# Moving the low part of a late expert weight on VectorE, in a fused graph layer and mixture of experts

## The reference, cut to what matters

```
deg = max((adj != 0).sum(-1), 1);  dinv = rsqrt(deg)
x = x + relu(((dinv * (adj + I) * dinv) @ ln(x) + ln(x)) @ Wg + bg)    # 4096 nodes, 256 features
xf = ln(x)
w, idx = top_k(softmax(xf @ Wr + br), 2);  w = w / w.sum()             # 16 experts
for e in range(16):
    h = gelu(xf @ W1[e] + b1[e])            # 256 -> 512
    y += combine[:, e] * (h @ W2[e] + b2[e])  # 512 -> 256, only where e is one of a token's two
return x + xf + y
```

## Time and profile before

| | |
|---|---|
| median of three runs | 624.11 us |
| profiled execution | 624.49 us, span 623.0 us, mean granted TensorE clock 0.98 |
| TensorE matmul / VectorE / ScalarE / GpSimd busy | 94% / 74% / 38% / 50% of the span |
| line 1213 (the late low parts) | 32 instructions, 331.1 to 450.3 us |
| line 1197 (`cut_low`, one a block) | 79 instructions, 92.1 us of idle time before them, ended by ScalarE's line 820 |
| line 1191 (one a block) | 79 instructions, 328.7 to 606.0 us |

### The profile page before, as it was taken

One profiled execution on the slowest core, in us unless ns is written; L12 is line 12 of the kernel. 1 busy time (PEld: TensorE's weight loads), 2 busy tenths in 40 slices (PEclk: granted clock), 3 DMA queues, 4 the chain that ended last, 5 costly groups with the idle time before them and its releaser, 6 DMA issues. The chain is left out here.

```text
span 623.0 us, 16840 instructions
## 1 busy us (share of the span) xinstructions
PE 582.5 (94%) x4756; PEld 462.4 (74%) x4756; DVE 460.7 (74%) x1469; ACT 236.9 (38%) x483; POOL 309.6 (50%) x361
## 2 busy tenths in 40 slices
PE   8899999999999999999748998999999999999992
PEld 7787888888888888888715665766667777777771
DVE  5776999999999999999755666666666656666561
ACT  3563334434444443433323444444433333333330
POOL 6343466666666666663342334534334444434443
PEclk9999999999999999999959999999999999999997
DMA  9978899999999999998548445766645443444420
GB/s 225 239 122 186 155 203 214 211 214 207 215 201 216 213 211 214 205 199 242 191 141 297 108 112 103 177 139 148 112 71 87 74 87 70 75 77 75 72 45 1
DMA packets 67605, 95.87 MB, mean 154 GB/s; under 512 B 9312, under 2 KB 42112, under 8 KB 67040
## 3 DMA queue, kind: packets, MB, share of 16 engines
q0 software_dynamic: 33408, 52.42, 48.9%
q1 hardware_dynamic: 32672, 40.88, 22.4%
q10 hardware_dynamic: 1472, 1.88, 0.9%
HBM read 103.71 MB, written 26.94 MB: 210 GB/s over the span
## 5 line engine op out<-in xcount | busy, mean ns | idle before, releaser
L505 PE MATMUL bank<-wall,at_xg 128*128 128x257 f16 x1024 | 238.7, 274 | 3.4 <-DVE at_xg L887 3.0
L507 PE MATMUL bank<-wall,at_xg 128*128 128x256 f16 x1024 | 233.4, 273 | 0.0
L1373 POOL DMA_INDIRECT out_dram<-orows,at_xg x79 | 123.5, 1563 | 162.1 <-DMA out_dram<-orows,at_xg 107.2
L1197 DVE SCALAR_TENSOR_TENSOR hl<-bank,xseT 128x512 f16<-128x512 f32 x79 | 54.6, 692 | 92.1 <-ACT xseT L820 92.1
L814 ACT ACTIVATE hgs<-hgs 128x512 f32<-128x512 f32 x79 | 49.8, 630 | 186.9 <-DVE hgs L1191 184.2
L631 PE MATMUL bank<-wall,feat 128*128 (+1 forms) x474 | 116.5, 383 | 2.5 <-DVE feat L1178 2.5
L505 PEld LDWEIGHTS bank<-wall,at_xg 128*128 128x128 f16 x1024 | 102.8, 100 | 20.1 <-DVE at_xg L887 6.8
L1341 POOL DMA_INDIRECT rows<-feat,posi x64 | 73.4, 1147 | 86.9 <-issue 82.2
L507 PEld LDWEIGHTS bank<-wall,at_xg 128*128 128x128 f16 x1024 | 100.2, 98 | 15.0
L657 PE MATMUL bank<-wall,xseT 128*128 (+1 forms) x632 | 108.3, 273 | 0.0
L887 DVE STREAM_TRANSPOSE at_xg<-abuf 128x512 int32<-128x512 int32 x128 | 87.0, 698 | 4.0 <-DVE abuf L879 0.3
(11 more groups left out here) (151 smaller groups left out, 768.1 us busy)
## 6 DMA issues: line engine op xcount, KB each, us to landing
abuf<-in_adj_dram POOLq DMA_DIRECT2D x128, 256.0 KB, 6.5
wst<-in_L_ffn_W_dram SPq DMA_DIRECT2D x32, 512.0 KB, 8.0
at_xg<-rows SPq DMA_DIRECT2D x79, 136.0 KB, 2.2
out_dram<-orows SPq DMA_DIRECT2D x32, 128.0 KB
abuf<-in_L_ffn_b_dram SPq DMA_DIRECT2D x4, 1024.0 KB, 8.0
wall<-in_x_dram SPq DMA_DIRECT2D x10, 256.0 KB, 11.7
rows<-pad POOLq DMA_DIRECT2D x11, 136.0 KB, 5.5
out_dram<-orows,at_xg POOLq DMA_INDIRECT x79, 3.8
```

The lines of the kernel that those rows point to most:

```text
L505: both = [lambda: pe.matmul(ps_acc[odd][:, 0:D + 1], w, yh[:, j, 0:D + 1], start=j == 0, stop=j == T - 1), lambda: pe.matmul(ps_acc[odd][: ...
L507: lambda: pe.matmul(ps_acc[odd][:, 0:D], w, yl[:, j, :], start=False, stop=False)]
L1197: V.scalar_tensor_tensor(out=hl[:, r % 2, :], in0=q_g[r % 2][:, :], scalar=SH, in1=hh[:, r % 2, :], op0=ALU.mult, op1=ALU.subtract).then_i ...
L1373: L.indirect_dma_start(out, bass.IndirectOffsetOnAxis(ap=info[r][:, 0:1].bitcast(U32), axis=0), orow[r], None, bounds_check=N - 1, oob_is_ ...
```

## The change

Both halves of a piece are made one block later: those of piece j in VectorE's steps 2j + 1 and 2j + 2, and within a step between the bias (line 1191) and `cut_low` (line 1197), where before they stood at the end of the step, behind `weigh`. The fetch of piece j + 2, which waits for them, moves on SyncE's queue from step 2j + 1 to step 2j + 2, and so behind one more fetch of tokens. `LATE` goes from 4 to 5, so that the last piece's second half, now in block 32, still falls in a round that is written out. ScalarE's high part stays where it was.

```diff
-LATE = 4
+LATE = 5
...
     def late(q, r):
 
-        return (U * q + r) // 2 if isinstance(q, int) and U * q + r < 4 * (E - EARLY) else None
+        return (U * q + r) // 2 if isinstance(q, int) and 0 <= U * q + r < 4 * (E - EARLY) else None
...
             if exists(*nxt):
                 load_block(*nxt)
-            if late(q, r) is not None and r % 2 and late(q, r) + 2 < 2 * (E - EARLY):
-                load_late(late(q, r) + 2)
+            prev = shift(q, r, -1)
+            if late(*prev) is not None and prev[1] % 2 and late(*prev) + 2 < 2 * (E - EARLY):
+                load_late(late(*prev) + 2)
...
             if exists(q, r):
                 bias1(q, r, e)
+            if late(*prev) is not None:
+                cut_low_late(late(*prev), prev[1] % 2)
             if exists(*prev):
                 cut_low(*prev)
             if exists(*prev2):
                 weigh(*prev2)
-            if late(q, r) is not None:
-                cut_low_late(late(q, r), r % 2)
```

## The result

The changed kernel takes 621.38 us (median of 19 runs, 618.65 to 625.26), the kernel before 625.41 us (19 runs, 623.41 to 628.01). The ratio is 0.9933, 95% interval 0.9919 to 0.9946: 4.2 us less, by the interval 3.4 to 5.1. I had expected 5.7 us less and a median of 618.4 us; 621.38 us lies just outside my forecast of 614.5 to 621.0 and inside the wider range of 613.5 to 622.0. The profiled execution took 618.88 us with a span of 617.4 us, where I had 618.8 and 617.3.

The account below looks back on a forecast made before the run. Ordered scatters were taken to bound up to block 16, VectorE blocks 16 to 32, TensorE after. Bias of 32 at 444.3 plus 1.2 us for piece 13 is 5.7 us earlier: 618.4 us, forecast 614.5 to 621.0, wider range 613.5 to 622.0.

Parts of the forecast that it names:

- rival B: Weight pieces or landings take more, at piece 13 and two others: gain only 2 to 3 us, 621.5 us; chance 0.19.
- The two regimes and the second brake: Second stage: VectorE paces blocks 16 to 32 (3.83 us), TensorE later ones (3.37); scatters 0 to 9, 4.76 each, brake earlier.
- rival A: Second stage: scatters don't bind and the whole VectorE gain comes through, about 14 us, 610 us; chance 0.09.
- The gap: VectorE's wait between bias and `cut_low`: low part fits with about 0.5 us cover left, step falls from 3.80 to 3.21 us.
- The head: VectorE's steps 0 and 1: waits of 1.1 and 0.6 us go, so scatter 0 comes 1.7 us earlier.
- Scatters 0 to 9 move as one piece: Blocks 0 to 16: the scatter chain hangs on landings alone and shifts 1.7 us, bias of 16 at 388.3 us.
- sign of being wrong: Scatters closer together in blocks 0 to 9, bias of 16 before 385 or after 391, or clock drop in 350 to 390 us.
- From 16 on: Blocks 16 to 32: TensorE's 3.37 us pace, but fetch 28 waits for scatter 20; bias of 27 at 427.4, of 32 at 444.3.
- rival C: Blocks 9 to 16: TensorE's clock falls to 1.2 GHz in short gaps, making the kernel slower, 630 us; chance 0.06.
- The fetch of piece 13: Behind fetch 28: the piece lands late, gelu 27 is 1.7 us late, 1.2 us reach the pace, bounds 0 and 3.8.
- The sum: Bias of 32 at 445.5 us instead of 451.24, 5.7 us earlier, all of it kept to the end: median 618.4 us.
- D: No change, 624.5 us: low parts hold up the nine scatters by the port rule, or `cut_low` starts later; chance 0.04.

Follow-up runs that it names:

- plain stores: Each indirect scatter-add replaced by a plain store to a spare buffer: in the kernel before ratio 0.9961, in the changed kernel 0.9738, both to the kernel before.
- pieces 8 to 15 only: The change for pieces 8 to 15 (blocks 17 to 32), old order for pieces 0 to 7: ratio to the kernel before 0.9892, second time 0.9880.
- changed, no fetches: The changed kernel without the weight fetches of pieces 2 to 15, all splits still made: ratio to the kernel before 0.9775.
- pieces 0 to 7 only: The change for pieces 0 to 7 (blocks 1 to 16), old order for pieces 8 to 15: ratio to the kernel before 1.0056.
- changed, again: The changed kernel as it is, timed a second time: ratio to the kernel before 0.9947.
- fetch first: The changed kernel with the weight fetch ahead of the token fetch in the same step of SyncE's queue: ratio to the kernel before 0.9925.
- before, again: The kernel before, unchanged, profiled once more: scatters 0 to 9 in 43.1 us, bias 0 to 16 in 62.4, 16 to 32 in 61.6.

## Why the prediction was right

What was right is the account of what bounds each stretch. Of the size, 5.7 us forecast, the runs gave 4.2 (3.4 to 5.1). The median fell into the stretch from 621.0 to 627.2 us, to which I had given 0.17, and next to rival B's 621.5.

*The two regimes and the second brake.* Right, and all else hangs on it. The full 14 us of rival A were there to be had (13.9 us between the kernels with plain stores; A's own sum comes to 14.8), and the scatters took most of them, which the row of TensorE's wait for tokens at block 16 had shown before the change.

*The gap.* Right: 0.58 us of cover left against 0.5 expected, pace 3.38 against 3.37.

*The head.* Right: scatter 0 at 337.66 us, expected at 337.7. Counted from the bias of 0 it is 1.7 us earlier in both profiles of each kernel (9.1 us in place of 10.7).

*Scatters 0 to 9 move as one piece.* This step failed in size. They took 43.85 us for 42.8 and the tenth landed later, so the token fetch of block 17 went out at 387.44 us and not at 385.4. Bias of 16: 390.64 us, expected 388.3. I had named the landings as the least certain term, with 4 us either way; the second profile of the changed kernel has 46.4 us, 3.6 more than before. The runs show why it went to the bad side: the moved fetch lengthens them. Counted from the bias of 0, the second profile puts the bias of 16 at 63.8 us, which would be 392.4 us in the first and past the 391 that I had named as a sign of being wrong.

*From 16 on.* The step in which fetch 28 waits for scatter 20 didn't hold up the bias of 27. That scatter started at 419.31 us, a little over a microsecond earlier, while block 16 was late; TensorE's pace alone gives the bias of 27, and TensorE waits for no tokens near it in either profile. What I hadn't counted is TensorE's clock. Busy time by stretch in the changed kernel (us, PE, PEld, DVE, ACT, POOL, PEclk, DMA share, GB/s):

```profile
384.00:388.00 4.00, 3.12 (x23) 1.99 (x21) 1.72 (x3) 2.00 (x3) 0.92 (x1) 1.00 0.74 153
388.00:390.00 2.00, 0.35 (x4) 0.35 (x5) 1.08 (x2) 0.06 (x1) 1.56 (x2) 0.85 0.38 88
390.00:392.00 2.00, 2.00 (x13) 1.63 (x11) 1.62 (x3) 0.64 (x2) 1.55 (x1) 0.50 0.82 267
392.00:394.00 2.00, 2.00 (x13) 1.35 (x12) 1.18 (x2) 1.53 (x2) 0.00 (x0) 0.80 0.96 178
```

and in the kernel before:

```profile
390.00:392.00 2.00, 2.00 (x18) 1.50 (x16) 0.82 (x3) 1.29 (x3) 1.21 (x1) 1.00 0.95 181
```

TensorE had waited 2.53 us for the tokens of block 17, and the clock fell to 0.50 (1.2 GHz) for about 3 us; the twelve matmuls of line 658 took 2.10 us in place of 1.31, and block 17 came 4.69 us behind block 16: 1.3 us lost. That is rival C in small, at one block and not at six, and it is one of my own signs of being wrong: a granted clock that drops in 350 to 390 us (the row from 388 us has 0.85). In the kernel before the wait was 1.47 us and the clock stayed. The Trainium skill, page "TensorE: Matmul & The Clock Gate", section "Part 1", has the clock halved after idleness; this trace agrees, and it came at the longest of its gaps.

But the length of the wait alone doesn't decide it, as the other profiles show. The clock also fell to 0.50 behind a wait of 3.31 us (first profile of pieces 8 to 15 only). Behind one of 2.24 us (changed, no fetches) a stretch of 2 us read 0.53, behind one of 1.93 us (pieces 0 to 7 only) one read 0.50. It stayed at 1.00 through waits of 2.26 us (changed, again), 2.79 us (fetch first) and 3.45 us (before, again). The last two, with the columns as above:

```profile
386.00:388.00 2.00, 0.00 (x0) 0.00 (x0) 0.07 (x1) 0.07 (x1) 1.33 (x1) 1.00 0.16 35
388.00:390.00 2.00, 1.31 (x14) 1.24 (x15) 0.87 (x2) 0.00 (x0) 1.70 (x2) 1.00 0.68 100
```

```profile
384.00:386.00 2.00, 0.00 (x0) 0.00 (x0) 1.31 (x3) 0.54 (x1) 1.70 (x2) 1.00 0.70 102
386.00:388.00 2.00, 0.98 (x11) 0.94 (x12) 0.54 (x2) 0.00 (x0) 0.74 (x1) 1.00 0.60 65
```

So the 1.3 us are what one execution lost, not a fixed price of the change; the second profile of the changed kernel has no fall up to block 16.

*The fetch of piece 13.* The right place, and a price that differs from run to run. In the first profile ScalarE waited for it, and the step took 3.89 us in place of 3.38.

```profile
429.59 1.06 ACT L811 ACTIVATE wall<-wst 128x1024 f16<-128x1024 f32 x1 [2.01 <-DMA wst<-in_L_ffn_W_dram]
430.56 0.61 ACT L815 ACTIVATE hgs<-hgs 128x512 f32<-128x512 f32 x1
```

That is 0.5 us, of which the next two steps (3.19 and 3.22 us) take back 0.35; 0.16 us stay, for the 1.2 that I had. In the second profile fetch 28 did wait long for scatter 20, as I had it. The fetch of piece 13 behind it was issued at 430.07 us, ScalarE waited 3.28 us, the chain that ended last runs through it, and the step took 5.34 us: 1.6 us stay.

```profile
430.07 0.43 SPq L389 DMA_DIRECT2D wst<-in_L_ffn_W_dram  x1
...
434.75 1.06 ACT L811 ACTIVATE wall<-wst 128x1024 f16<-128x1024 f32 x1 [3.28 <-DMA wst<-in_L_ffn_W_dram]
```

ScalarE's waits for pieces 4 to 7, 3.2 to 5.0 us for three of them, I had called cheap; fetch first takes them away and gains nothing that can be told.

*The sum.* Bias of 32 at 446.19 us, expected 445.5. I had block 16 2.3 us too early and left out 1.3 us for the clock; against that stand 2.0 us for a switch of experts that didn't bind and 1.0 too much for piece 13. The errors offset each other by chance. The 19 runs give 4.2 us and not 5.7. The two profiles of each kernel point the same way: from the bias of 0 to that of 32 the changed kernel takes 117.6 and 120.3 us, the kernel before 122.6 and 124.0.

*The rivals.* B, more lost to fetches and landings, is nearest to the median of the runs. It happened at the scatters in both profiles, and at piece 13 too in the second. What I had held against B was wrong: before, fetches did not go out at like points of the scatters, but two of five 2.0 and 3.4 us into one, as the table of single scatters shows. D fell: `cut_low` starts as before, and a scatter still holds GpSimd 1.55 us (1564 ns on average against 1563).

## What to carry to other kernels

Before pricing a gap that is filled, look for the chain that runs slower than the engine's new pace but is still hidden by buffers; a single short wait for data at one block can be its only trace. An edit that pays in one stretch can cost in another where another chain sets the time, so price it by stretch and apply it only there. A transfer that moves with the edit counts by what it runs beside and from when on: here the weight fetches cost the nine scatters 1 to 3 us in the old step and 3 to 6 us in the moved one.

## What the runs showed that was not expected

- Nine ordered scatters of 128 rows take 40.5 to 40.9 us with no weight fetch beside them, 42.0 to 43.2 with five of 512 KB in the old step, 43.9 to 46.4 with these one step later (where in four of the five profiles the fifth is issued only behind the start of scatter 9).
- TensorE's clock fell to 0.50 after a wait of 2.5 us in the middle of a busy stage in one profile, and stayed at 1.00 (2.4 GHz) after one of 3.45 us at the like place of another.
- With plain stores the changed kernel's blocks start 3.38 us apart from block 3 to block 32 without a deviation (the bias of 32 at 107.8 us behind that of 0).
